# Second attention of a fused transformer kernel: the first norm on ScalarE, ranked values copied once per eight tiles, transposed rows moved by a transfer

## What is computed

```python
def _layernorm(x, axis=-1, eps=1e-05):
    m = jnp.mean(x, axis=axis, keepdims=True)
    v = jnp.var(x, axis=axis, keepdims=True)
    return (x - m) / jnp.sqrt(v + eps)

def _L1_xattn_ref(x, content_embeddings, Wq, bq, Wk, bk, Wv, bv, Wo, bo):
    queries = x @ Wq.T + bq
    keys = content_embeddings @ Wk.T + bk
    values = content_embeddings @ Wv.T + bv
    attn = jax.nn.softmax(jnp.einsum('bqc,bkc->bqk', queries, keys) * scale, axis=-1)
    attended = jnp.einsum('bqk,bkc->bqc', attn, values)
    out = x + attended
    return out @ Wo.T + bo

def _L1_ffn_ref(x, router_w, router_bias, ...):       # 32 experts, the best 4 of each token
    logits = flat @ router_w.T + router_bias
    scores = jax.nn.softmax(logits, axis=-1)
    topk_scores, topk_idx = jax.lax.top_k(scores, TOPK)
    ...

x = x + _L0_ffn_ref(_layernorm(x), ...)                       # its sum is finished in the second attention
x = x + _L1_xattn_ref(_layernorm(x), ctx_1024, ctx_1024, ...)  # first norm: xn
x = x + _L1_ffn_ref(_layernorm(x), ...)                        # second norm: xm
```

## Time and profile before

| | |
|---|---|
| Runs | 1448.69, 1449.73, 1450.63 us |
| Median | 1449.73 us |
| Span of the profiled execution | 1446.9 us (the time of the whole execution is not listed apart for it; the span is 2.8 us below the median) |
| Second attention in the span | about 806 to 944.5 us |
| Clock granted to TensorE there | 0.59 from 805 to 830, 1.00 from 830 to 927.5, 0.92 to 944.5 |

### The profile page before, as it was taken

The page is one execution under the profiler, slowest core; times in us unless marked ns, Lnnn a source line. Parts: engine busy times, 40 slices in busy tenths (PEclk is TensorE's granted clock), DMA queues, the critical chain, the costliest instruction groups (busy, mean ns, idle before and its releaser), DMA issues. The chain is left out here.

```text
span 1446.9 us, 29194 instructions
## 1 busy us (share of the span) xinstructions
PE 1322.9 (91%) x7743; PEld 1053.3 (73%) x7744; DVE 777.4 (54%) x2053; ACT 589.1 (41%) x1314; POOL 648.1 (45%) x873
## 2 busy tenths in 40 slices
PE   7988999999879999999999499947999999989994
PEld 4666777777558888888888377714888888848883
DVE  4874888887742222222222588784233333337774
ACT  2454777777322222222222266625433333322110
POOL 1213565665113333333332255403655555257775
PEclk9998999999799999999999699956999999999998
DMA  2107322222731111111111665353555555845554
GB/s 95 59 30 307 114 89 90 80 93 99 289 120 44 51 51 51 51 51 51 51 51 36 207 194 175 117 236 120 185 161 162 163 162 152 131 124 160 161 165 131
DMA packets 108684, 175.75 MB, mean 121 GB/s; under 512 B 16698, under 2 KB 83275, under 8 KB 105292
## 3 DMA queue, kind: packets, MB, share of 16 engines
q1 hardware_dynamic: 72276, 96.09, 19.5%
q0 software_dynamic: 20736, 56.65, 14.7%
q10 hardware_dynamic: 15608, 22.25, 4.3%
HBM read 115.13 MB, written 59.77 MB: 121 GB/s over the span
## 5 line engine op out<-in xcount | busy, mean ns | idle before, releaser
L1228 POOL DMA_INDIRECT xg<-t_xn,token x160 | 151.4, 946 | 154.7 <-PE psum L2088 69.3
L2162 POOL DMA_INDIRECT su_yg<-t_y,slot x128 | 124.2, 970 | 68.4 <-issue 37.5
L2100 PE MATMUL psum<-gu,m_xT 128*128 x640 | 153.3, 383 | 0.0
L1403 DVE TENSOR_TENSOR m_h<-psum,m_h 128x512 f32<-128x512 f32 x72 | 49.7, 690 | 163.7 <-ACT m_h L1378 163.7
L1465 PE MATMUL psum<-w,m_hT 128*128 x576 | 136.4, 380 | 0.8 <-ACT m_hT L1384 0.8
L2100 PEld LDWEIGHTS psum<-gu,m_xT 128*128 128x128 f32 x640 | 116.5, 192 | 13.0 <-issue 0.2
L1444 PE MATMUL psum<-w,m_xT_high 128*128 x288 | 120.5, 419 | 0.0
L2059 DVE TENSOR_TENSOR m_h<-psum,m_sg 128x256 f32<-128x256 f32 x80 | 33.9, 424 | 159.0 <-ACT m_sg L2038 159.0
L1444 PE MATMUL psum<-w,m_xT_low 128*128 x288 | 114.4, 397 | 0.0
L1444 PE MATMUL psum<-w_low,m_xT_high 128*128 x288 | 113.7, 395 | 0.0
L1465 PEld LDWEIGHTS psum<-w,m_hT 128*128 128x128 f32 x576 | 103.8, 190 | 12.4 <-issue 1.2
(11 more groups left out here) (305 smaller groups left out, 3119.8 us busy)
## 6 DMA issues: line engine op xcount, KB each, us to landing
t_y<-m_y SPq DMA_DIRECT2D x80, 256.0 KB, 2.2
w<-in_w SPq DMA_DIRECT2D x8, 1024.0 KB, 11.4
t_x<-at_x SPq DMA_DIRECT2D x64, 128.0 KB, 1.9
t_w_low<-at_low ACTq DMA_DIRECT2D x64, 128.0 KB, 1.7
w_low<-t_w_low SPq DMA_DIRECT2D x8, 1024.0 KB, 13.3
at_yg<-t_y SPq DMA_DIRECT2D x32, 256.0 KB, 2.8
gu<-in_gu ACTq DMA_DIRECT2D x8, 1024.0 KB, 12.4
w<-in_x SPq DMA_DIRECT2D x16, 256.0 KB, 2.7
```

The source lines that it names most:

```text
L1228: pool.indirect_dma_start(out=g.xg1[j % GB][:, k * D:(k + 1) * D], out_offset=None, in_=g.xn4, in_offset=bass.IndirectOffsetOnAxis(ap=g.to ...
L2100: last = pe.matmul(ps_gu[p][:, k * 2 * M1:(k + 1) * 2 * M1], xT[p][:, at:at + P], g.gu[:, bass.ds(ex[k] * (DC * 2 * M1) + c * 2 * M1, 2 * ...
L2162: pool.indirect_dma_start(out=yg[p][k][:, :], out_offset=None, in_=g.y1, in_offset=bass.IndirectOffsetOnAxis(ap=g.slot[:, at:at + 1], axis ...
```

## The change

Three edits of `attention1_phase`:

1. The first norm is applied by ScalarE with `apply_scalar`, in a new stage XA = 2, behind the copies of stage 8 in ScalarE's order. GpSimd makes the shift that it needs. VectorE's `apply` at the head of its step goes, and so does the special case for tile 0.
2. `top` and `ix` become arrays for eight tiles, and are copied to `top_v` and `top_i` once in eight tiles.
3. ScalarE's second copy out of PSUM, to `xn4T`, goes. SP moves `xmT` to `xn4T` by a transfer, behind its store of `xm`; ScalarE waits, before it writes an `xmT` buffer, until the transfer of two tiles before has landed (`xmT_st`). `xm_out` is signalled after the copy to `xmT`.

```diff
+        RANKED = 8
...
-        lg, top, ix = ring("lg", [P, E1]), ring("top", [P, 8]), ring("ix", [P, 8], U32)
+        lg, top, ix = ring("lg", [P, E1]), sb("top", [P, 8 * RANKED]), sb("ix", [P, 8 * RANKED], U32)
...
-        SUM, XN, S, PT, WO, XM, R, TOP = 1, 3, 4, 5, 6, 8, 9, 10
+        SUM, XA, XN, S, PT, WO, XM, R, TOP = 1, 2, 3, 4, 5, 6, 8, 9, 10
...
         def _(sp):
...
                     sp.wait_ge(xm_done, t.n + 1)
                     sp.dma_start(g.xn4[rows(t), :], xm[p][:, :]).then_inc(xm_st[p], 16)
+                    sp.wait_ge(xm_out, t.n + 1)
+                    sp.dma_start(g.xn4T[:, :].rearrange("p (c n) -> p c n", c=DC)[:, :, rows(t)],
+                                 xmT[p][:, :].rearrange("p (c n) -> p c n", c=DC)).then_inc(xmT_st[p], 16)
...
-            for st in xm_st:
+            for st in (*xm_st, *xmT_st):
                 sp.wait_ge(st, NT // 2 * 16)
...
         def _(pool):
...
                     lna.invert(pool, t)
+                    lna.shift(pool, t)
...
         def _(dve):
...
-                if (t := stage(s, XN)) is not None and not (t.loop is None and t.off == 0):
-                    wait(dve, x_t, t.shift(-1).n)
-                    lna.apply(dve, x2[t.mod(8)][:, :], xn[t.mod(2)][:, :], t).then_inc(xn_done, 1)
...
-                    dve.max(top[p][:, :], lg[p][:, :]).then_inc(top_done, 1)
+                    dve.max(top[:, ranked_at(t)], lg[p][:, :]).then_inc(top_done, 1)
...
-                if (t := ranked) is not None:
-                    p = t.mod(2)
-                    dve.tensor_copy(g.top_v[:, bass.ds(t.n * 8, 8)], top[p][:, :])
+                if (t := ranked) is not None and t.mod(RANKED) == RANKED - 1:
+                    at = bass.ds(t.shift(1 - RANKED).n * 8, RANKED * 8)
+                    dve.tensor_copy(g.top_v[:, at], top[:, :])
                     dve.wait_ge(ix_done, t.n + 1)
-                    dve.tensor_copy(g.top_i[:, bass.ds(t.n * 8, 8)], ix[p][:, :])
+                    dve.tensor_copy(g.top_i[:, at], ix[:, :])
...
-                if s.loop is None and s.off == SUM:
-                    first = At(None, 0, 0)
-                    lna.apply(dve, x2[0][:, :], xn[0][:, :], first).then_inc(xn_done, 1)
...
         def _(act):
...
                     wait(act, r_mm, t.shift(-1).n)
-                    act.activation(xmT[p][:, :], ps_m[:, 0:D], ACT.Copy)
-                    act.activation(g.xn4T[:, :].rearrange("p (c n) -> p c n", c=DC)[:, :, rows(t)],
-                                   ps_m[:, 0:D].rearrange("p (c n) -> p c n", c=DC), ACT.Copy).then_inc(xm_out, 1)
+                    wait(act, xmT_st[p], t.div(2).n * 16)
+                    act.activation(xmT[p][:, :], ps_m[:, 0:D], ACT.Copy).then_inc(xm_out, 1)
+                if (t := stage(s, XA)) is not None:
+                    wait(act, x_t, t.shift(-1).n)
+                    lna.apply_scalar(act, x2[t.mod(8)][:, :], xn[t.mod(2)][:, :], t).then_inc(xn_done, 1)
```

More of the change, by code:

```diff
@@ L1501, in attention1_phase @@
         x3_st, xm_st = [sem(f"x3_st{i}") for i in range(4)], [sem(f"xm_st{i}") for i in range(2)]
+        xmT_st = [sem(f"xmT_st{i}") for i in range(2)]
         s_y = [sem(f"s_y{i}") for i in range(GB)]
@@ L1525, in logits_of, with ranked_at @@
             return ps_s[t.mod(2)][:, P:P + E1]
+        def ranked_at(t):
+            return slice(t.mod(RANKED) * 8, (t.mod(RANKED) + 1) * 8)
         @block.sync
@@ L1620, in step @@
                     wait_alone(dve, top_done, t.n + 1, passed[0])
-                    dve.max_index(ix[p][:, :], top[p][:, :], lg[p][:, :]).then_inc(ix_done, 1)
+                    dve.max_index(ix[:, ranked_at(t)], top[:, ranked_at(t)], lg[p][:, :]).then_inc(ix_done, 1)
                 if (t := into) is not None:
```

## The result

The changed kernel takes 1440.45 us, the median of four runs (1437.07 to 1447.97), against 1449.21 of the kernel before. The ratio is 0.9941, 95% interval 0.9923 to 0.9959: faster by 0.6%. The forecast was 1439.9 us with a range of 1437 to 1446. The profiled execution is the slowest of the four, 1447.97 us, so its page must be read with care: it shows a price that the other runs pay in part only.

The account below looks back on a forecast made before the run. Bound: a loop of mutual waits between TensorE and VectorE in the second attention. Terms -8.8 - 1.0 + 0.3 + 0 - 0.3 = -9.8 us from the median 1449.73 gave 1439.9 us, range 1437 to 1446.

Parts of the forecast that it names:

- The loop: Second attention: TensorE's xn transposes and VectorE's add wait for each other each step; moving the norm early cuts this.
- The floor: Steady part of the second attention: TensorE's own need per step, taken as 3.36 us.
- (a): First reading of TensorE's need: the regular step less idle time at the weight load, 3.61 - 0.23 = 3.38 us.
- (b): Second reading: first step without an xn transpose, 3.08 us, plus 0.27 for the pair of xn transposes, 3.35.
- a sign of being wrong: Steady part: ScalarE waiting for landed stores was listed among observations that would show the forecast wrong.
- the rival with 10%: ScalarE's norm of xm waits for late-landing stores, cutting the gain: 3.53 us a step, 1444.3 us; chance 10%.
- the term of the steady part: 26 steps of the second attention at 3.36 us, 87.4 instead of 96.13: -8.8 us.
- The ramp: Steps ahead of the steady part: -1.0 us for waits for xn; at the very start +0.3, bounds -0.5 to +1.
- The table load: At the start, ScalarE's 1.28 us load for the exponential follows tile 1's norm, ending about the same time, 817.1.
- The copies: VectorE's small copies of ranked values, made once per eight tiles: counted 0, as VectorE has time to spare.
- The transfer: SP's extra 128 KB per step to xn4T: nothing waits; DMA load 0.41 us by bytes or 0.95 by packets.
- The end of the phase: Last steps: part of ScalarE's copy goes, about 0.3, against SP's wait for the last landing; together -0.3 us.

Follow-up runs that it names:

- e8: Kernel before, with VectorE keeping the norm of xn but one step earlier, ahead of its residual add; no other edit: ratio 0.9952 to the kernel before.
- e11: e1 with ScalarE's norm of xn moved back into the step of its transposes (stage 3): ratio 1.0076 to the kernel before.
- e1: Kernel before plus only the first edit, the norm of xn on ScalarE one step early: ratio 0.9924 to the kernel before.
- e5: The changed kernel measured and profiled again, unaltered: ratio 0.9938 to the kernel before, median 1439.54 us of 6 runs.
- e4: The changed kernel with its third edit undone, so ScalarE copies to xn4T and no transfer: ratio 0.9929 to the kernel before.
- e9: The changed kernel with four buffers for xm, two of them in the array gu, transfer kept: ratio 0.9931 to the kernel before.
- e10: The changed kernel with four buffers for xm and without the transfer, ScalarE copying to xn4T: ratio 0.9904 to the kernel before.
- e12: The same kernel as e4 once more, on the chip of e9 to e11: ratio 0.9926 to the kernel before.
- e2: Kernel before plus only the second edit, ranked values copied once per eight tiles: ratio 1.0004 to the kernel before.
- e3: Kernel before plus only the third edit, xmT moved to xn4T by a transfer, norm left on VectorE: ratio 1.0006 to the kernel before.
- e13: e10's kernel (four buffers for xm, no transfer) measured again: ratio 0.9915 to the kernel before.
- e14: The changed kernel once more, unaltered, in the group with e13: ratio 0.9946 to the kernel before.

## Why the prediction was right

**The loop, and what TensorE needs by itself.** Right. L1755 waits for nothing, and e8 and e11 show the loop by opening it without the engine and closing it without the old one. The floor was put at 3.36 from two readings (3.38 and 3.35) and is 3.30; e1 shows what that is worth in 26 steps, 86.12 us against 87.4, 1.3 to the good. The rows of before and after show where the readings are long. For (a), what went is more than the 0.23 idle at the weight load: from the start of L1741 to that of the `xn` transposes it was 0.76 us (855.34 to 856.10) and is 0.47 in e5 (848.85 to 849.32). For (b), the same step read from `xm` transposes to `xm` transposes, 927.23 to 930.27 in the kernel before, is 3.04 instead of 3.08, and with the 0.27 gives 3.31. ScalarE at some 80% (79% in e5) and the share of 0.75 came as said. VectorE did not: it was to fall below 80% and is at 84% in e5 (73.99 of 88 us), and its wait for L1776 was to grow to 0.6 and is 0.39. The rows of e5 show it:

```profile
849.97 0.46 DVE L1631 SCALAR_TENSOR_TENSOR at_x<-at_yg,weight,at_x 128x256 f32<-128x256 f32 x1
850.47 0.43 DVE L132 BATCH_NORM_STATS2 at_lna_stats<-at_x 128x6 f32<-128x256 f32 x1
851.29 0.42 DVE L1647 TENSOR_TENSOR at_x<-psum,at_x 128x256 f32<-128x256 f32 x1 [0.39 <-PE psum L1776]
```

VectorE gets back less than the busy time of what is taken from it, and TensorE's step is shorter than forecast. The norm was counted with 0.41, its duration, but from its start to that of the next instruction it is 0.33 (855.63 to 855.96 in the step of the earlier trace rows). The two copies were worth 0.05: from the start of the sum L1631 to that of the statistics it is 0.50 us now and was 0.55 with them between (856.77 to 857.32), where the statistics wait for the sum either way. So 3.30 - 0.39 = 2.91 us of each step are VectorE's, where 2.84 was counted with the copies still in. Over the stretch the wait for L1776 is 7.5 us in e5, less than the 9.3 before.

**Late stores.** ScalarE waiting for landed stores in the steady part was named as a sign of being wrong, and it came true: 7.0 us in the first profile, 5.6 in e5. This was the rival with 10%, and it is there beside the forecast, in part. It was put as a bound on every step that takes over beyond a landing of 3.5 us. The median rose from 1.8 to 2.4, and single ones to 4.1, so it strikes single steps: 1.9 us in e5, and 4.5 in the first profile with the fall of the clock. What the rival lacked are SP's long issues, at which stores start or land late. The cost takes back what the lower floor gave: the term of the steady part, -8.8, is -8.2 in e5 (87.97) and -4.2 in the first profile.

**The ramp.** This is the term that was sized worst: forecast -1.0 and +0.3, with bounds of -2.1 and +1 in sum. From VectorE's first memset to the first `xm` transposes it was 24.97 us before, 25.07 in the first profile and 22.04 in e5. The two profiles of the changed kernel differ in TensorE's granted clock, 0.50 and 0.61 in the mean from 805 to 830; the kernel before has 0.59. So at a like clock the term is -2.9, and it is lost where the clock stays low. Four other kernels with the norm early on ScalarE (e4, e9, e10, e12) take 21.93 to 22.01, e2 and e3, with the norm late on VectorE, 24.39 and 24.79. The forecast counted two waits of TensorE for `xn`, 0.81 each. The trace before has two more in the ramp behind the very first, 1.03 at 816.97 and 0.66 at 822.56, and e5 has none of the four. The table load, in ScalarE's timeline of the first profile after:

```profile
815.09 0.60 ACT L154 ACTIVATE at_xn<-at_x,at_lna_less,at_lna_rstd 128x256 f32<-128x256 f32 x1 [1.10 <-POOL at_lna_less L148]
815.71 1.28 ACT L1688 ACT_TABLE_LOAD   x1
817.00 0.33 ACT L1688 ACTIVATE at_pr<-psum,at_nmx 128x77 f32<-128x77 f32 x1
```

The exponential starts 0.01 us after the load's end, at 817.00 where it was 817.10; in e5 it starts 0.05 after it. The Trainium skill, "ScalarE: Activation LUTs", section "What ACT_TABLE_LOAD costs", counts 1.38 us of drain beside the 1.28: the trace shows none here, neither ahead of the load (the norm ends at 815.69) nor behind it, and the measurement decides.

**The copies.** Counted 0; e2 has 1.0004, no change within an interval of 0.17% either way.

**The transfer.** Counted as neutral for itself: e3 has 1.0006, at the old step of 3.61. At the new step it makes more of the waits for stores above. Its load was priced at 0.41 us a step by bytes and 0.95 by packets; it is 0.47, near the price by bytes, and the share in the changed kernel, 0.75, is the 0.74 forecast. So the trace agrees with the Trainium skill's "DMA: Bandwidth & Descriptors", "Specifications", where 512 B are the least for the line rate; with smaller pieces nothing was run here. SP's issue takes 0.63 and not the 0.43 of the nearest row. The end of the phase is as late after the 27th transposes as before (17.78 us against 17.57, -0.3 forecast): from the last maximum of VectorE to the end of its last copy it is 1.01 us (939.03 to 940.04) where it was 0.80; the copies are of 64 columns now. The copy saved on ScalarE does not show. In both the next phase follows 0.3 us behind the last copy (0.27 and 0.28), so no landing of a transfer was in the way.

**The sum.** For e5, from VectorE's first memset in the phase to the first transfer of the next: 138.67 before (806.13 to 944.80), 127.79 now (807.30 to 935.09), -10.9 against -9.8 forecast: -2.9 in the ramp, -8.2 in the 26 steps and +0.2 behind them. Of that 1.2 us are lost ahead of the phase and 0.3 behind, and the spans differ by 9.4 us. The right total is thus made of a floor that was too high (1.3 us), a ramp that gave 2.2 more than forecast, an end that gave 0.5 less, waits for stores that took some 1.9 (87.97 against e1's 86.12), and 1.5 us outside the phase that no term had. The mechanism was right; that the total fits to 0.6 us is luck in part, since these errors cancel.

## What to carry to other kernels

When two engines each wait for the other once a step, look for the loop in their written order and take out of it an operation whose inputs are ready a step ahead. In this kernel the engine that does it was secondary (0.9952 against 0.9924), and in the late place moving it to ScalarE made the kernel slower (1.0076). Read the floor from a step that lacks the waiting operation, between two starts of the same instruction, and check every wait of the ramp as well as of the steady part. Shorter steps use up the slack of double buffers behind stores: check the landing time against the ring before the step shrinks, and count buffers by the longest landing, not by the median.

## What the runs showed of the hardware that was not expected

Small idle stretches of TensorE can be followed by a loss longer than themselves: behind 0.75 and 0.94 us of waiting the granted clock was 0.54 (888.5 to 891.5), the transposes took 0.69 us for 0.38 and a step 4.96 for 3.30. In e5 waits of 0.41 and 0.78 us were not followed by such a fall. The ramp too goes with the clock: the first profile of the changed kernel, e8 and e13 have a granted clock of 0.50 from 805 to 830, and their first step behind it takes 4.58 to 4.91 us; that of e1, e4, e5, e9, e10, e12 and e14 takes 3.35 or 3.36.

The issue of a load or a store, 0.35 to 0.45 us of SP as a rule, takes over 1 us once or a few times in the phase, in every profile: once in the kernel before (1.28 at 814.93), three times between 840 and 881 in both the first profile of the changed kernel (up to 1.91) and e5 (up to 1.57), and in e10, without the transfer, up to 1.61. In the changed kernel, with the DMA engines 0.75 loaded, waits for late stores and long steps follow such issues; in e9, with four buffers, none do.

The kernel before takes 1448 to 1450 us in the first measurement and beside e5 and e8, and 1522 to 1526 in the other three groups. In the one profile compared, that of e2, the 75 us are in the last phase. That phase, which lasts 185.9 us in the first profile of the kernel before (1261.0 to 1446.9, DMA share 0.50, 147 GB/s), has this row:

```profile
1262.00:1523.40 261.40, 181.32 (x690) 137.40 (x688) 116.65 (x239) 32.88 (x72) 123.72 (x128) 0.88 0.36 109
```

It is 261.4 us at a DMA share of 0.36 and a granted clock of 0.88, while the regular steps of the second attention are the same 3.61 us in both. That this goes with the chip is not shown: the four groups ran on chips numbered 9, 8, 14 and 8, and number 8 stands at 1448 us as well as at 1522. Why was not tried.
